# Low parts of the values in the zero columns of their weights, in a cross-attention kernel on one Trainium2 core

## The chip, the cores and the metric

The kernel runs on one core of a Trainium2 chip. The metric is the time on the device in microseconds (us) of one execution; lower is better. The core has TensorE (PE in the rows; PEld is its weight load), VectorE (DVE), ScalarE (ACT), GpSimd (POOL) and the DMA queue of SyncE (SP). Each runs its own list of instructions in order, and semaphores tie the lists together. Before the change the kernel takes 660.38 us, the median of three runs.

## The reference, cut to what matters

The input is 4 batches of 512 tokens of width 1024. A LoRA layer with a router updates them (first phase of the kernel). Then each batch attends to its own 64 vision tokens with 32 heads of width 32, and a layer norm follows:

```python
Q = (hidden_states @ Wq.T + bq).reshape(B, L, NH, HD)
K = (vision_features @ Wk.T + bk).reshape(B, Vn, NH, HD)
Vv = (vision_features @ Wv.T + bv).reshape(B, Vn, NH, HD)
scores = jnp.einsum('blhd,bvhd->bhlv', Q, K) / np.sqrt(HD).astype(np.float32)
scores = jnp.where(mask, scores, -jnp.inf)
attn = jax.nn.softmax(scores, axis=-1)
ctx = jnp.einsum('bhlv,bvhd->blhd', attn, Vv).reshape(B, L, H)
attn_out = ctx @ Wo.T + bo
x = hidden_states + attn_out
# layer norm of x over the 1024 columns, times ln_g plus ln_b
```

All of it is float32. TensorE works here in float32r, which keeps fewer bits, so a product a·b is made of parts: a = a_hi + a_lo, b = b_hi + b_lo, and a_hi·b_hi + a_hi·b_lo + a_lo·b_hi is summed in PSUM: three matmuls for one.

## The kernel before

Two phases are written out as one list of stages that every engine walks (`first_phase`, `second_phase`, `run`). The first phase makes the updated tokens, the queries, the keys and the values, and stores queries, keys, values and output weights, each in high and low parts, in DRAM. The second phase, from about 320 us on, is a software pipeline of 86 steps.

A unit is 256 tokens (8 units), and a chunk is 4 heads (128 columns) of a unit, so a unit has 8 chunks and there are 64 chunks in all. Below, s is the step and c = s mod 8 is its place in a group of eight steps. Chunk n passes these stations:

- scores(n), TensorE, step n+2: queries times the block-diagonal keys, 6 matmuls into one bank (two banks in turn).
- scale_and_min(n), VectorE, step n+2: L921 scales and masks, L926 takes the minima. GpSimd then subtracts (L1220) and ScalarE takes the exponentials (L1138, L1142).
- inverse(n), VectorE, step n+3: sums (L931) and reciprocal (L934). GpSimd multiplies (L1213).
- p_transposed(n), TensorE, step n+5: four transposes (L730). ScalarE makes the high parts p_hi (L1147), VectorE the low parts p_lo (L938).
- context(n), TensorE, step n+6 (L735 to L743): probabilities times values. For each of two pairs g of heads the weights `vbd[:, c, g, :]` are 128 rows (2 heads by 64 vision tokens) by 128 columns. Of these only the 64 columns of the pair's own two heads are filled, 64·g to 64·g+63; the rest stays zero from a memset (L1208). Three matmuls for each g add into the same 256 columns of a bank, so all 128 rows of the result are filled: 6 matmuls.
- ctx_high(n), ScalarE, first in step n+7 (L1156), adds the bias of the values and rounds to cx_hi. ctx_low(n), VectorE (L943), in step n+7 between inverse and p_low, makes cx_lo.

In each step TensorE does scores, p_transposed, half a group of the output projection (12 matmuls of 512 columns, `projection`) and context, in this order. At c = 6 and c = 7 the projection is the first group of the unit whose chunks were last finished. It waits for `clo_done`, the counter of finished cx_lo: at c = 6 for the first four chunks of the unit, at c = 7 for all eight, and the eighth chunk's context was made by TensorE only at c = 5, so its parts are made in step c = 6.

VectorE in each step does L921, L926, L931, L934, L943 and L938. In even steps it adds the output group to the residual (L951, L955); at c = 2 and 6 follow the moments (L959) and at c = 3 and 7 a Newton step in five small instructions (L963 to L977), one of which (L970) multiplies two SBUF tensors. Stages of the layer norm go to ScalarE (L1160, L1163, L1170) and to GpSimd, one in each step (gain L1228, shift L1233), behind its two operations of the softmax. Output groups begin at step 14 and residuals at step 16; chunks end with context(63) in step 69.

Of the kernel before, what the change touches and what calls it, by code (L numbers as in the profile page):

```python
# [5 lines left out]
F32 = mybir.dt.float32  # L6
# [184 lines left out]
def xattn_kernel(nc, xT, ctxT, mask, BT, rW, rb, WqT, WkT, WvT, biases, WoT, ln_g, ln_b, out):  # L191
# [15 lines left out]
    with ExitStack() as ctx:  # L207
# [11 lines left out]
        bias_c = sb("bias_c", [P, 4, KC])  # L219
        bq_c, bk_c, bv_c, bo_c = (bias_c[:, k, :] for k in range(4))  # L220
# [57 lines left out]
        vbd = [at(f"vbd{n}", [P, KC, 2, P], AT_B + 16384 + 8192 * k, F32R) for k, n in enumerate(("_hi", "_lo"))]  # L278
# [24 lines left out]
        ps_v = [ps[:, 0, 0:U], ps[:, 1, 0:U]]  # L303
# [40 lines left out]
        pv_mm, chi_done, clo_done = sem("pv_mm"), sem("chi_done"), sem("clo_done")  # L344
# [21 lines left out]
        def _(sp):  # L366
# [122 lines left out]
            def load_values(b, half):  # L489
                cs = slice(4 * half, 4 * half + 4)  # L490
                for l in range(2):
                    for g in range(2):
                        for s in range(2):
                            sp.dma_start(vbd[l][64 * s:64 * s + 64, cs, g, 64 * g + HD * s:64 * g + HD * s + HD].bitcast(F32),
                                         v_heads[l, b, g, s][:, cs, :]).then_inc(v_in[half], 16)
# [36 lines left out]
            def step(s):  # L532
# [3 lines left out]
                if s in (1, 2):  # L536
                    sp.wait_ge(zeroed, 4)
# [43 lines left out]
        def _(pe):  # L581
# [153 lines left out]
            def context(n):  # L735
# [3 lines left out]
                wait(pe, clo_done, n - 1)  # L739
                if n == 0:  # L740
                    pe.wait_ge(q_copied, ALL - 4)
                three(ps_v[c % 2], [(vbd[0][:, c, g, :], vbd[1][:, c, g, :], p_hi[c % 2][:, g, :], p_lo[c % 2][:, g, :])
                                    for g in range(2)]).then_inc(pv_mm, 1)  # L743
# [33 lines left out]
        def _(dve):  # L777
# [162 lines left out]
            def ctx_low(n):  # L940
                c, u = n % KC, n // KC % 2
                dve.wait_ge(chi_done, n + 1)
                dve.scalar_tensor_tensor(cx_lo[u][:, c, :], ps_v[c % 2], bv_c[:, c:c + 1], cx_hi[u][:, c, :],  # L943
                                         ALU.add, ALU.subtract).then_inc(clo_done, 1)
# [34 lines left out]
            def step(s):  # L979
# [5 lines left out]
                if live(s - 7, CHUNKS):  # L985
                    ctx_low(s - 7)
# [30 lines left out]
        def _(act):  # L1017
# [130 lines left out]

            def ctx_high(n):
                c, u = n % KC, n // KC  # L1150
                act.wait_ge(pv_mm, n + 1)
# [4 lines left out]
                act.activation(cx_hi[u % 2][:, c, :], ps_v[c % 2], ACT.Identity, bias=bv_c[:, c:c + 1]).then_inc(chi_done, 1)  # L1156
# [15 lines left out]
            def step(s):  # L1172
                c = s % KC
                if live(s - 7, CHUNKS):
                    ctx_high(s - 7)
                if live(s - 5, CHUNKS):
                    p_high(s - 5)
                if live(s - 2, CHUNKS):
                    exponential(s - 2)
                for at_c, stage_, n in ((2, inverse_deviation, tile_at(s, 0, 2)), (4, normalise, tile_at(s, 0, 2)),  # L1180
# [10 lines left out]
        def _(pool):  # L1191
# [13 lines left out]
            def zero():  # L1205
                pool.wait_ge(bound_ready, ALL)
                for z in (kbd[0], kbd[1], vbd[0], vbd[1]):
# [77 lines left out]
```

## Time and profile before

| | us |
|---|---|
| median of three runs | 660.38 (660.12 to 660.53) |
| the profiled execution | 661.26 |
| its span, from first to last instruction | 659.5 |
| TensorE busy | 643.9 (98%) |
| VectorE busy | 478.5 (73%) |
| ScalarE busy | 320.4 (49%) |
| GpSimd busy | 204.6 (31%) |

A busy TensorE counts overlapping matmuls as one stretch, so its work is better read from the distance between the starts of its instructions. An instruction's duration is likewise longer than the distance to the next one where the two overlap. A bracket at the end of a row of the timeline is the idle time of the engine before that row and who ended it. The shares over the whole span mix the two phases; those of the second phase are read by windows.

### The profile page before, as it was taken

The page shows a single profiled execution, that of the slowest core. Times are in us where ns is not written, and L with a number is a line of the kernel's source. Part 1 is how long each engine was busy: PE and PEld are TensorE (multiplying, and loading weights), DVE is VectorE, ACT ScalarE, POOL GpSimd, SP SyncE. Part 2 cuts the span into 40 slices and gives each one's busy share as a digit, 9 for nine tenths or more (in the row PEclk, how much of TensorE's full clock was granted, in tenths as well). Part 3 has the DMA queues.
Part 4 walks back from the last instruction along what each step waited for, and adds up shares of the span by engine and source line. Part 5 has one row for each costly group of instructions (what it writes and reads, how often), then busy time and mean ns, then how long its engine had stood idle before and what let it go on. Part 6 is the DMA issues. An engine that isn't in the chain of part 4 may idle for free.

```text
span 659.5 us, 10610 instructions
## 1 busy us (share of the span) xinstructions
PE 643.9 (98%) x3559; PEld 558.7 (85%) x3559; DVE 478.5 (73%) x917; ACT 320.4 (49%) x935; POOL 204.6 (31%) x215
## 2 busy tenths in 40 slices
PE   7999999999999999999999999999999999999995
PEld 6988879888888878888888989898888889888884
DVE  5779985578447773677467777988888888988634
ACT  5453362223242242323267666766676676766411
POOL 0020001100110002000433334666565656656643
PEclk9999999999999999999999999999999999999998
DMA  8936684436883478612866982515444443512311
GB/s 304 378 126 177 178 305 141 176 80 209 244 298 98 109 239 266 261 33 103 227 217 231 413 282 79 172 59 171 113 131 136 132 132 111 176 68 94 129 64 64
DMA packets 103253, 114.12 MB, mean 173 GB/s; under 512 B 56992, under 2 KB 76064, under 8 KB 103200
## 3 DMA queue, kind: packets, MB, share of 16 engines
q1 hardware_dynamic: 103008, 113.20, 52.3%
q8 instruction: 28, 0.46, 0.3%
q10 hardware_dynamic: 192, 0.26, 0.2%
q14 instruction: 25, 0.20, 0.1%
HBM read 67.29 MB, written 46.14 MB: 172 GB/s over the span
## 4 chain that ended last, share of the span: by engine, by line
PE 83%; DVE 11%; DMA 2%; ACT 2%; issue 1%; SPq 1%; DVEq 0%; ACTq 0%
PE ps L585 24%; PE ps L586 24%; PE ps L587 24%; PE ps L647 4%; PE ps L730 4%; DVE w_lo L803 2%; DVE h_t L890 1%; DMA stage<-WkT 1%; DVE x_sb L873 1%; DVE h_t L887 1%; DVE act_lo L858 1%; PE ps L657 1%; DVE q_sb L900 1%; ACT act_hi L1103 1%; DMA x_sb<-xT 1%
## 5 line engine op out<-in xcount | busy, mean ns | idle before, releaser
L585 PE MATMUL ps<-wo_hi,cx_hi 128*128 128x512 f32 x256 | 104.5, 408 | 0.0
L1138 ACT ACTIVATE s_sb<-s_sb,s_min 128x64 f32<-128x64 f32 x256 | 86.1, 337 | 34.2 <-DVE s_min L926 34.2
L585 PE MATMUL ps<-act_hi,w_hi 128*128 128x512 f32 x256 | 100.9, 394 | 1.6 <-DVE kv_sb L813 0.9
L587 PE MATMUL ps<-wo_hi,cx_lo 128*128 128x512 f32 x256 | 100.3, 392 | 0.0
L586 PE MATMUL ps<-wo_lo,cx_hi 128*128 128x512 f32 x256 | 100.2, 391 | 0.0
L586 PE MATMUL ps<-act_lo,w_hi 128*128 128x512 f32 x256 | 99.8, 390 | 0.0
L587 PE MATMUL ps<-act_hi,w_lo 128*128 128x512 f32 x256 | 99.8, 390 | 0.0
L1202 POOL TENSOR_TENSOR u_sb<-a_sb,w_sb 128x512 f32<-128x512 f32 x16 | 18.1, 1153 | 240.7 <-DVE w_sb L847 234.0
L1220 POOL TENSOR_TENSOR s_sb<-s_sb,s_min 128x256 f32<-128x256 f32 x64 | 39.3, 614 | 133.5 <-DVE s_min L926 133.5
L921 DVE SCALAR_TENSOR_TENSOR s_sb<-ps,mask_f 128x512 f32<-128x512 f32 x64 | 44.2, 690 | 46.9 <-PE ps L587 45.4
L1103 ACT ACTIVATE act_hi<-h_t 128x512 fp32r<-128x512 f32 x32 | 20.3, 633 | 114.1 <-DVE h_t L890 114.1
L1213 POOL TENSOR_TENSOR s_sb<-s_sb,s_inv 128x512 f32<-128x512 f32 x64 | 66.9, 1046 | 0.0
L585 PEld LDWEIGHTS ps<-act_hi,w_hi 128*128 128x128 f32 x256 | 48.1, 188 | 12.0 <-issue 1.3
L587 PEld LDWEIGHTS ps<-wo_hi,cx_lo 128*128 128x128 f32 x256 | 48.1, 188 | 10.3
L587 PEld LDWEIGHTS ps<-act_hi,w_lo 128*128 128x128 f32 x256 | 48.1, 188 | 10.2
L586 PEld LDWEIGHTS ps<-act_lo,w_hi 128*128 128x128 f32 x256 | 48.1, 188 | 9.2
L586 PEld LDWEIGHTS ps<-wo_lo,cx_hi 128*128 128x128 f32 x256 | 48.3, 189 | 8.5
L585 PEld LDWEIGHTS ps<-wo_hi,cx_hi 128*128 128x128 f32 x256 | 48.2, 188 | 8.3
L1147 ACT ACTIVATE p_hi<-ps 128x512 fp32r<-128x512 f32 x64 | 38.1, 595 | 29.3 <-PE ps L730 29.1
L585 PE MATMUL ps<-u_hi,b_hi 128*128 128x512 f32 x128 | 49.9, 390 | 0.0
L587 PE MATMUL ps<-u_hi,b_lo 128*128 128x512 f32 x128 | 49.8, 389 | 0.0
L586 PE MATMUL ps<-u_lo,b_hi 128*128 128x512 f32 x128 | 49.8, 389 | 0.0
(117 smaller groups left out, 1514.2 us busy)
## 6 DMA issues: line engine op xcount, KB each, us to landing
q_cols<-q_sb SPq DMA_DIRECT2D x32, 512.0 KB, 3.3
qb<-q_cols SPq DMA_DIRECT2D x64, 256.0 KB, 3.5
x_sb<-xT SPq DMA_DIRECT2D x32, 256.0 KB, 3.3
h_rows<-hn_sb SPq DMA_DIRECT2D x64, 128.0 KB, 3.0
output_weights<-wo_sb SPq DMA_DIRECT2D x32, 256.0 KB, 2.5
z_sb<-h_rows SPq DMA_DIRECT2D x16, 512.0 KB, 4.1
out<-z_sb SPq DMA_DIRECT2D x15, 512.0 KB, 2.8
stage<-WvT SPq DMA_DIRECT2D x8, 512.0 KB, 4.8
```

The lines of the kernel that those rows point to most:

```text
L585: pe.matmul(dst, lh, rh, start=(first and j == 0), stop=False)
L586: pe.matmul(dst, lh, rl, start=False, stop=False)
L587: mm = pe.matmul(dst, ll, rh, start=False, stop=(last and j == n - 1))
L647: mm = pe.matmul(ps_al[:, t, :], x_sb[:, k, t * P:(t + 1) * P], a_rhs[:, k, :], start=(k == 0), stop=(k == KC - 1))
L730: mm = pe.transpose(ps_t[c % 2][:, g, t * P:(t + 1) * P], s_sb[c % 4][:, HPC * t + 2 * g:HPC * t + 2 * g + 2, :].rearrange("p h v -> p (h ...
L921: dve.scalar_tensor_tensor(s_sb[c % 4][:], ps_s[c % 2].rearrange("p (h v) -> p h v", v=V), -SCALE, mask_f[:, n // 16, :].unsqueeze(1).to_b ...
L1103: act.activation(act_hi[:, c, :], h_t[m % 3][:], ACT.Copy).then_inc(hhi_done, 1)
L1138: act.activation(s_sb[c % 4][:, h, :], s_sb[c % 4][:, h, :], ACT.Exp, bias=s_min[c % 2][:, h:h + 1], scale=-1.0, accum_out=s_sum[c % 2][:, ...
L1147: act.activation(p_hi[n % 2][:], ps_t[n % 2], ACT.Copy).then_inc(phi_done, 1)
L1202: pool.tensor_tensor(u_sb[t % 2][:], a_sb[:, t, :].unsqueeze(1).to_broadcast([P, NR, R]), w_sb[:, t, :].unsqueeze(2).to_broadcast([P, NR, ...
L1213: pool.tensor_tensor(s_sb[c % 4][:], s_sb[c % 4][:], s_inv[c % 2][:].unsqueeze(2).to_broadcast([P, TU * HPC, V]), ALU.mult).then_inc(p_rea ...
L1220: pool.tensor_tensor(rest, rest, s_min[c % 2][:, ACT_HEADS:].unsqueeze(2).to_broadcast([P, TU * HPC - ACT_HEADS, V]), ALU.subtract).then_i ...
```

## The change: what it does

The weights of the context hold both parts: for the pair g, the 64 columns that were zero get the low parts of the same values. One pass with p_hi and one with p_lo then give, for each g, the product with the high parts in the 64 rows of that g and the product with the low parts in the other 64 rows. The two pairs no longer add into the same columns but take 256 columns each, so the bank's 512 columns are in use, and 4 matmuls take the place of 6 (the product of both low parts, left out before, is among them).

The two halves have to be added across partitions. In step n+7, ScalarE first copies the whole bank to SBUF (`ctx_copy`, 128x512). VectorE, where ctx_low stood, does `ctx_sum`: two instructions on 64 partitions each. For pair g it reads the high half from PSUM in its own partitions, and the bias and the low half from SBUF in the other 64 partitions, and writes `cx_sum` in its own. ScalarE then rounds `cx_sum` to cx_hi (`ctx_high`, now behind the exponentials of the step), and GpSimd makes cx_lo (`ctx_low`, now last in its step). TensorE's context waits for the sums of chunk n−2 and no longer for its low parts; the projection still waits for `clo_done`. One of four memsets goes, and the DMAs of the values write the same bytes to one tile. On the host the halves of each 128 values of the bias are swapped.

```diff
-        vbd = [at(f"vbd{n}", [P, KC, 2, P], AT_B + 16384 + 8192 * k, F32R) for k, n in enumerate(("_hi", "_lo"))]
+        vbd = at("vbd", [P, KC, 2, P], AT_B + 16384, F32R)
+        cx_raw = [at(f"cx_raw{k}", [P, 2, U], AT_B + 24576 + 2048 * k) for k in range(2)]
+        cx_sum = [at(f"cx_sum{k}", [P, U], AT_B + 28672 + 1024 * k) for k in range(2)]
...
-        ps_v = [ps[:, 0, 0:U], ps[:, 1, 0:U]]
+        ps_v = [ps[:, k, :].rearrange("p (g n) -> p g n", g=2) for k in range(2)]
...
-                            sp.dma_start(vbd[l][64 * s:64 * s + 64, cs, g, 64 * g + HD * s:64 * g + HD * s + HD].bitcast(F32),
+                            col = 64 * (g ^ l) + HD * s
+                            sp.dma_start(vbd[64 * s:64 * s + 64, cs, g, col:col + HD].bitcast(F32),
                                          v_heads[l, b, g, s][:, cs, :]).then_inc(v_in[half], 16)
...
-                wait(pe, clo_done, n - 1)
+                wait(pe, cx_summed, 2 * (n - 1))
...
-                three(ps_v[c % 2], [(vbd[0][:, c, g, :], vbd[1][:, c, g, :], p_hi[c % 2][:, g, :], p_lo[c % 2][:, g, :])
-                                    for g in range(2)]).then_inc(pv_mm, 1)
+                for g in range(2):
+                    pe.matmul(ps_v[c % 2][:, g, :], vbd[:, c, g, :], p_hi[c % 2][:, g, :], start=True, stop=False)
+                    mm = pe.matmul(ps_v[c % 2][:, g, :], vbd[:, c, g, :], p_lo[c % 2][:, g, :], start=False, stop=True)
+                mm.then_inc(pv_mm, 1)
...
-            def ctx_low(n):
-                c, u = n % KC, n // KC % 2
-                dve.wait_ge(chi_done, n + 1)
-                dve.scalar_tensor_tensor(cx_lo[u][:, c, :], ps_v[c % 2], bv_c[:, c:c + 1], cx_hi[u][:, c, :],
-                                         ALU.add, ALU.subtract).then_inc(clo_done, 1)
+            def ctx_sum(n):
+                c = n % KC
+                dve.wait_ge(cx_copied, n + 1)
+                wait(dve, chi_done, n - 1)
+                wait(dve, clo_done, n - 1)
+
+                for g in range(2):
+                    own, other = slice(64 * g, 64 * g + 64), slice(64 - 64 * g, 128 - 64 * g)
+                    dve.scalar_tensor_tensor(cx_sum[n % 2][own, :], ps_v[c % 2][own, g, :], bv_c[other, c:c + 1],
+                                             cx_raw[n % 2][other, g, :], ALU.add, ALU.add).then_inc(cx_summed, 1)
...
+            def ctx_copy(n):
+                act.wait_ge(pv_mm, n + 1)
+                wait(act, cx_summed, 2 * (n - 1))
+                act.activation(cx_raw[n % 2][:], ps_v[n % 2], ACT.Copy).then_inc(cx_copied, 1)
+
             def ctx_high(n):
                 c, u = n % KC, n // KC
-                act.wait_ge(pv_mm, n + 1)
+                act.wait_ge(cx_summed, 2 * n + 2)
...
-                act.activation(cx_hi[u % 2][:, c, :], ps_v[c % 2], ACT.Identity, bias=bv_c[:, c:c + 1]).then_inc(chi_done, 1)
+                act.activation(cx_hi[u % 2][:, c, :], cx_sum[n % 2][:], ACT.Copy).then_inc(chi_done, 1)
...
                 if live(s - 7, CHUNKS):
-                    ctx_high(s - 7)
+                    ctx_copy(s - 7)
                 if live(s - 5, CHUNKS):
                     p_high(s - 5)
                 if live(s - 2, CHUNKS):
                     exponential(s - 2)
+                if live(s - 7, CHUNKS):
+                    ctx_high(s - 7)
...
+            def ctx_low(n):
+                c, u = n % KC, n // KC % 2
+                pool.wait_ge(chi_done, n + 1)
+                pool.tensor_tensor(cx_lo[u][:, c, :], cx_sum[n % 2][:], cx_hi[u][:, c, :], ALU.subtract).then_inc(clo_done, 1)
...
                     if c == at_c and live(n, TILES - 1):
                         stage_(n, half)
+                if live(s - 7, CHUNKS):
+                    ctx_low(s - 7)
```

## Rows read from the trace of the kernel before

**Rows 1.** The page, part 1: busy time, share of the span, instructions.
```profile
PE 643.9 (98%) x3559; PEld 558.7 (85%) x3559; DVE 478.5 (73%) x917; ACT 320.4 (49%) x935; POOL 204.6 (31%) x215
```

**Rows 2.** Windows: length, busy PE, PEld, DVE, ACT, POOL; clock, DMA share, GB/s.
```profile
376.00:380.00 4.00, 4.00 (x27) 3.60 (x27) 3.86 (x8) 3.76 (x18) 2.40 (x3) 1.00 1.02 415
...
460.00:500.00 40.00, 40.00 (x247) 35.81 (x246) 34.16 (x74) 28.02 (x104) 25.52 (x27) 1.00 0.45 130
```

**Rows 3.** Timeline of TensorE, steps c = 2 and 3: start, duration, engine, line.
```profile
485.71 0.60 PE L730 MATMUL ps<-ident,s_sb 128*128 128x128 f32 x4
...
488.90 0.28 PE L585 MATMUL ps<-p_hi,vbd_hi 128*128 128x256 f32 x1
...
489.61 0.28 PE L585 MATMUL ps<-kbd_hi,qb 128*128 128x256 f32 x1
...
490.33 0.60 PE L730 MATMUL ps<-ident,s_sb 128*128 128x128 f32 x4
...
490.69 0.48 PE L585 MATMUL ps<-wo_hi,cx_hi 128*128 128x512 f32 x1
```

**Rows 4.** Timeline of VectorE, steps c = 2 and 3.
```profile
485.91 0.69 DVE L921 SCALAR_TENSOR_TENSOR s_sb<-ps,mask_f 128x512 f32<-128x512 f32 x1 [1.70 <-PE ps L587]
...
487.24 0.41 DVE L931 TENSOR_REDUCE s_sum<-s_sb 128x4 f32<-128x256 f32 x1
487.68 0.20 DVE L934 RECIPROCAL s_inv<-s_sum 128x8 f32<-128x8 f32 x1
487.80 0.43 DVE L943 SCALAR_TENSOR_TENSOR cx_lo<-ps,bias_c,cx_hi 128x256 fp32r<-128x256 f32 x1
488.15 0.68 DVE L938 TENSOR_TENSOR p_lo<-ps,p_hi 128x512 fp32r<-128x512 f32 x1
...
489.47 0.69 DVE L955 BATCH_NORM_STATS2 stats<-z_sb 128x6 f32<-128x512 f32 x1
490.19 0.21 DVE L959 BATCH_NORM_AGGREGATE mv<-stats 128x2 f32<-128x12 f32 x1
490.53 0.69 DVE L921 SCALAR_TENSOR_TENSOR s_sb<-ps,mask_f 128x512 f32<-128x512 f32 x1
...
494.05 0.85 DVE L970 TENSOR_TENSOR rstd<-nudge,guess 128x1 f32<-128x1 f32 x1
494.94 0.21 DVE L977 TENSOR_SCALAR offset<-mv,rstd 128x1 f32<-128x1 f32 x1
```

**Rows 5.** Lines of the source: ns shortest/median/longest, first and last start.
```profile
L943 DVE SCALAR_TENSOR_TENSOR cx_lo<-ps,bias_c,cx_hi x64: 432/433/484, 347.2 to 630.2; 128x256 fp32r<-128x256 f32 x64
...
L970 DVE TENSOR_TENSOR rstd<-nudge,guess x16: 158/856/861, 401.6 to 655.3; 128x1 f32<-128x1 f32 x16
...
L1147 ACT ACTIVATE p_hi<-ps x64: 576/597/602, 337.4 to 622.8; 128x512 fp32r<-128x512 f32 x64
...
L1142 ACT ACTIVATE s_sb<-s_sb x64: 399/403/407, 328.5 to 613.4; 128x256 f32<-128x256 f32 x64
```

**Rows 6.** Timeline of GpSimd, steps c = 2 and 3.
```profile
487.40 0.61 POOL L1220 TENSOR_TENSOR s_sb<-s_sb,s_min 128x256 f32<-128x256 f32 x1 [1.75 <-DVE s_min L926]
487.97 1.05 POOL L1213 TENSOR_TENSOR s_sb<-s_sb,s_inv 128x512 f32<-128x512 f32 x1
488.98 1.29 POOL L1228 TENSOR_TENSOR z_sb<-z_sb,g_b 128x512 f32<-128x512 f32 x1
...
493.59 1.29 POOL L1233 TENSOR_TENSOR z_sb<-z_sb,lb_b 128x512 f32<-128x512 f32 x1
```

**Rows 7.** Timeline of the first phase: GpSimd, then VectorE, in the same stretch.
```profile
31.74 3.03 POOL L1202 TENSOR_TENSOR u_sb<-a_sb,w_sb 128x512 f32<-128x512 f32 x2 [30.24 <-DVE w_sb L847]
...
31.98 3.87 DVE L803 TENSOR_TENSOR b_lo<-stage,b_hi 128x1024 fp32r<-128x1024 f32 x2 [0.33 <-ACT b_hi L1050]
```

**Rows 8.** Timeline of TensorE at the scores of step 16.
```profile
383.08 0.28 PE L587 MATMUL ps<-p_hi,vbd_lo 128*128 128x256 f32 x1
383.25 0.39 PE L585 MATMUL ps<-kbd_hi,qb 128*128 128x256 f32 x1
```

More of the change, by code:

```diff
@@ L343, in xattn_kernel @@
         pt_mm, phi_done, plo_done = sem("pt_mm"), sem("phi_done"), sem("plo_done")
-        pv_mm, chi_done, clo_done = sem("pv_mm"), sem("chi_done"), sem("clo_done")
+        pv_mm, cx_copied, cx_summed = sem("pv_mm"), sem("cx_copied"), sem("cx_summed")
+        chi_done, clo_done = sem("chi_done"), sem("clo_done")
         o_mm, z_ready, bn_done, ag_done = sem("o_mm"), sem("z_ready"), sem("bn_done"), sem("ag_done")
@@ L536, in step @@
                 if s in (1, 2):
-                    sp.wait_ge(zeroed, 4)
+                    sp.wait_ge(zeroed, 3)
                     load_values(0, s - 1)
@@ L985, in step @@
                 if live(s - 7, CHUNKS):
-                    ctx_low(s - 7)
+                    ctx_sum(s - 7)
                 if live(s - 5, CHUNKS):
@@ L1206, in zero @@
                 pool.wait_ge(bound_ready, ALL)
-                for z in (kbd[0], kbd[1], vbd[0], vbd[1]):
+                for z in (kbd[0], kbd[1], vbd):
                     pool.memset(z[:].bitcast(F32), 0.0).then_inc(zeroed, 1)
@@ L1265, in by_blocks, with by_halves @@
         return a.reshape(*a.shape[:-1], P // B, KC, B).swapaxes(-3, -2).reshape(a.shape)
+    def by_halves(a):
+        return np.asarray(a).reshape(KC, 2, P // 2)[:, ::-1].reshape(H)
     arrays = {
@@ L1274 @@
         "biases": lay(np.stack([np.asarray(b).reshape(KC, P) for b in
-                                (L1_xattn_bq, L1_xattn_bk, L1_xattn_bv, by_blocks(L1_xattn_bo))]), 2, 0, 1),
+                                (L1_xattn_bq, L1_xattn_bk, by_halves(L1_xattn_bv), by_blocks(L1_xattn_bo))]), 2, 0, 1),
         "WoT": lay(L1_xattn_Wo, 1, 0),
```

## The prediction

> **What bounds the kernel now.** I read the page's busy shares first, then the second phase by windows, then one stretch of two steps on each engine's timeline. TensorE is busy for 98% of the span [rows 1] and for 40.00 of 40.00 us in the middle of the second phase, where VectorE has 34.16 and GpSimd and ScalarE about two thirds [rows 2]. The reader should see two things there. TensorE has no idle time at all, so each matmul that goes is time that can come out. And VectorE, at 85% of the same window, is next: TensorE may get faster by about a seventh at most before VectorE is the bound, and this change loads VectorE.
>
> One step of TensorE is 4.62 us, transposes to transposes (485.71 to 490.33), of which the six context matmuls take 488.90 to 489.61: 0.71, or 0.118 each [rows 3]. Eight steps (a unit) take 36.96.
>
> VectorE's part of a step: 2.24 from its first instruction to p_low, which lasts 0.68; residual steps go on to the end of L955 at 4.25; at c = 2 and 6 the moments end at 4.49; at c = 3 and 7 the Newton step ends at 4.62 [rows 4]. Measured to the next possible start, each is about 0.08 shorter, since an instruction that depends on nothing may start 0.08 before the one ahead ends (reciprocal 487.68 + 0.20, next start 487.80). Four steps: 4.17 + 2.84 + 4.41 + 4.54 = 15.96; a unit: 31.9 of 36.96. The idle 1.70 ahead of 485.91 is that slack [rows 4].
>
> **What the change removes.** Two of six context matmuls in each of 64 steps: 2 x 0.118 = 0.237, so a step of TensorE is 4.38, a unit 35.06, and all 64 are worth 15.2 us if nothing else ends last. The copies, the rounding and GpSimd's part have room as work. ScalarE is busy 28.02 of 40 [rows 2], 3.24 a step; it gains a copy of 128x512 from PSUM, priced like L1147 (0.60), and the rounding now reads SBUF (like L1142, 0.40) instead of 0.46 from PSUM [rows 5]: 3.8 of 4.4. GpSimd has 25.52 of 40, 2.95 a step, and gains a subtraction of 128x256 that no row shows in this form: at least 0.61 (L1220, same size with a broadcast) and at most 1.29 (L1228, twice the size) [rows 6]. I take 1.29 x 0.61 / 1.05 = 0.75, the size scaled as L1220 to L1213. That makes 3.7. The new waits between them: VectorE's sums wait for the copy, with p_low and the residual queued behind; copy and L1147 are 1.2 us of work at the head of ScalarE's step, and the sums come at 2.0. ScalarE's rounding waits for the sums, with the layer norm and the next copy behind; the sums are done at 3.0, before the exponentials are.
>
> **What it costs VectorE.** One instruction of 256 columns becomes two, also of 256 columns; half the partitions should save nothing. No row shows an instruction that starts on other partitions than its neighbours, so the price is bounded. If the two overlap as L943 does now, the second adds its distance, 488.15 − 487.80 = 0.35 [rows 4]. If none of the three changes of partitions (reciprocal to first sum, first to second, second to p_low) lets the next start before the last has ended, then each start waits for the end plus about 0.035 (L931 at 487.24, 0.41 long, to its dependent at 487.68) [rows 4]. From the reciprocal's start to p_low it is 0.47 now. It becomes 0.24 + 0.47 + 0.47 = 1.18 with a sum of 0.43, or 1.28 with 0.48, the longest L943, which started behind idle time [rows 5]. The extra is 0.71 to 0.82. I take 0.76: the pairs that overlap in the rows all start on partition 0, so they say least about these three, and a gain below nothing is excluded, since an instruction is added.
>
> The Trainium skill, "VectorE: DVE Perf Modes", section "Two Vector instructions with no wait between them", has a rule here. An instruction is held until all earlier ones have finished when its operand or output starts in another group of 32 partitions than the last one used in that memory. By it the three holds are certain and the sum is the one with 0.76; without it the sum would be the first rival's. No row of before can show it.
>
> The extra counts in full at c = 0, 1, 2, 4, 5, 6. At c = 3 and 7 it is mostly absorbed: L970, which lasts 0.158 alone, now takes 0.856 [rows 5], and at c = 3 it ends at 494.90, when GpSimd's shift ends (493.59 + 1.29) [rows 4, 6]. It waits for that operation. Coming 0.76 later, at 4.28 into its step, it would end at 4.44 instead of 4.37: +0.07. VectorE's unit is then 31.9 + 6 x 0.76 + 2 x 0.07 = 36.6. That is more than TensorE's 35.06: VectorE becomes the bound, and a unit gains 0.36 us, not 1.9.
>
> **Where TensorE waits.** At c = 7 the projection needs the low parts made in step c = 6, and the chain there is longer: copy, sums, rounding behind the exponentials, then GpSimd last in its step. From VectorE's start of the step GpSimd ends its gain at 490.27 − 485.91 = 4.36 [rows 4, 6]. Its subtraction starts 0.04 before that, as its operations now follow each other, and ends at 5.07; the rounding is done well before, at about 3.6. TensorE wants it one step plus 0.16 after that start (490.69 against 490.53) [rows 3, 4]: 4.38 + 0.13 = 4.51, with 0.06 for the signal. So there is a stall of 0.62 plus whatever VectorE lags behind. Queued behind that wait on TensorE are the rest of the projection, the context and the next scores. In the first unit with residuals (steps 16 to 23) the lag grows by 0.55 at c = 0 (4.17 + 0.76 − 4.38), falls by 0.78 at c = 1 and so to nothing, grows by 0.79 and 0.23 at c = 2 and 3, and after c = 4 and 5 is 0.79 at c = 6: a stall of 1.4 and a unit of 36.47. After that VectorE never idles and a unit is 36.6, of which 1.54 is this stall.
>
> **The sum**, against the profiled execution of 661.26 us:
> - Steps 6 to 15, no residuals: VectorE has room (2.92 + 0.76 against 4.38), so 10 x 0.237 = 2.4 comes out. Against it, the scores of step 16 start 0.17 after the matmul before them instead of 0.12, and take 0.39 instead of 0.28 [rows 8], with the DMA engines full (1.02) just before [rows 2]: I read that as the queries' load only just landing. TensorE would come 2.4 earlier; the load follows only in part. Between 0 and 2.4 is lost; I take 1.0, nearer to nothing because the weights' loads ahead of it are released by TensorE's progress. Net 1.4.
> - Steps 16 to 63: 0.49 + 5 x 0.36 = 2.3.
> - Steps 64 to 69: 6 x 0.237 = 1.4; VectorE is light again. At step 71 the last chunk's chain (0.60, 0.48, 0.48, 0.40, 0.75 and five signals of about 0.05: 2.95) meets a half group of about 2.8 less the overlap of the last matmul: 0.4 lost. Net 1.0.
> - The memset that goes and the regrouped DMAs cost or bring nothing: TensorE works through that stretch on queries.
>
> Together 4.7: 656.6 for the profiled execution. That one stood 0.9 above the median of its runs, so the median goes to 655.7.
>
> **Rivals.**
> First, the sums overlap like the rest. Then VectorE's unit is about 31.9 + 6 x 0.35 = 34.0 and it has slack; TensorE's is 35.06 plus the bare stall of 0.62, 35.7. For it: every independent pair in the rows overlaps. Against it: none of those pairs changes partitions. Saved: 1.4 + 6 x 1.26 + 1.0 = 10.0, so 650.4.
>
> Second, and slower: the arbitration at L970. In the changed kernel GpSimd has its new subtraction queued directly behind the shift at c = 3 and 7. If GpSimd keeps its turn, L970 waits for both and ends at 5.07 instead of 4.44: +0.63 twice a unit, 1.26, and over six units 7.5, which gives 663.2. It decides from 0.8 us a unit on. Against it stands one place in the first phase. Two GpSimd operations of about 1.04 each were queued together from 31.74 and took 3.03 in all, with VectorE's two-input L803 starting at 31.98 [rows 7]: VectorE got in between the two.
>
> Third, four matmuls take as long as six, because something other than their count sets the pace. Then TensorE keeps 36.96 and gains a stall of about 0.3 a unit: 662. The distances are so even at 0.118 that I give it little.
>
> **How the numbers follow.** Forecast 0.60, first rival 0.20, second 0.12, third 0.03, and 0.05 for an extra on VectorE above 0.85, where the unit passes 36.96 by more than the other steps bring. Within the forecast, an extra of 0.71 gives a unit of 36.2 and 653.4, one of 0.82 gives 37.1 and 658.5, and the load of the queries moves it by 1 more: 652.4 to 659.5. The range reaches down to the first rival and a little above the forecast's own: 649.8 to 661.0. A measurement of this kernel can tell about 0.2% (1.3 us) from no change. Faster by more than that (below 659.1): 0.57 of the forecast and 0.20 less a little, so 0.73. Within: 0.12. Slower: 0.12 and 0.03 from the second and third rivals and the tail, 0.15.
>
> **What would show it.** In the changed kernel's profile: context matmuls still 0.12 apart, four in a step; on VectorE the reciprocal's start to p_low's at 1.2 to 1.3 us (0.8 would be the first rival), and no idle time ahead of L921 in the units with residuals; one wait of TensorE a unit at c = 7, of 1.3 to 1.7 us, for GpSimd's low part (0.6 under the first rival); L970 ending within 0.1 of the shift's end (0.7 later under the second); and 36.6 us from unit to unit. The prediction is wrong above all if the three changes of partitions cost other than 0.71 to 0.82 together: each 0.1 there moves the time by about 4.

## The result, and the profile after

The changed kernel takes 668.82 us (median of 4 runs, 668.29 to 669.21), the kernel before 660.25 (4 runs, 659.72 to 660.53): a ratio of 1.013, 95% interval 1.012 to 1.015. It is slower, where 655.7 was forecast. The profiled execution took 668.49 us, its span is 666.7 us against 659.5.

The page of the changed kernel, parts 1 and 5, answers to [rows 1]:

```profile
PE 636.1 (95%) x3431; PEld 546.6 (82%) x3431; DVE 519.1 (78%) x981; ACT 339.9 (51%) x999; POOL 248.5 (37%) x278
...
L592 PE MATMUL ps<-wo_hi,cx_hi 128*128 128x512 f32 x256 | 106.8, 417 | 16.2 <-POOL cx_lo L1247 16.2
```

TensorE is busy 7.8 us less, for 128 matmuls fewer, and stands idle for 16.2 us ahead of the output projection, waiting for GpSimd's low parts. That is half of the 15.1 that 128 x 0.118 make. Part of the rest went back in at a lower clock, as the windows show (columns as in [rows 2]):

```profile
380.00:382.00 2.00, 2.00 (x7) 1.52 (x7) 1.89 (x5) 1.57 (x9) 1.52 (x2) 0.59 1.07 327
382.00:384.00 2.00, 2.00 (x7) 1.57 (x6) 0.69 (x1) 0.48 (x2) 0.82 (x2) 0.55 1.07 347
456.00:458.00 2.00, 2.00 (x5) 1.62 (x6) 1.90 (x6) 1.91 (x7) 0.60 (x2) 0.50 0.94 317
458.00:460.00 2.00, 2.00 (x8) 1.57 (x8) 1.90 (x5) 1.50 (x8) 2.00 (x3) 0.78 0.10 39
...
460.00:500.00 40.00, 38.24 (x230) 33.73 (x229) 37.75 (x81) 28.66 (x104) 29.44 (x34) 1.00 0.44 126
```

In the window of 40 us VectorE went from 34.16 [rows 2] to 37.75 and TensorE from 40.00 to 38.24. VectorE has no idle time there to speak of (of the 2.25 us, 0.26 stand at 461.48, right behind a stretch at the lower clock, and the rest are gaps of about 0.04 between its instructions), so it is the bound. The first four windows have a granted clock of 0.50 to 0.78: in each of them it stood for a part or all of the time at 0.5, which is the 1.2 GHz level.

TensorE's timeline at c = 6 and 7, which answers to [rows 3]:

```profile
490.75 0.28 PE L750 MATMUL ps<-p_hi,vbd 128*128 128x256 f32 x1
490.87 0.28 PE L751 MATMUL ps<-p_lo,vbd 128*128 128x256 f32 x1
490.99 0.28 PE L750 MATMUL ps<-p_hi,vbd 128*128 128x256 f32 x1
491.11 0.28 PE L751 MATMUL ps<-p_lo,vbd 128*128 128x256 f32 x1
491.23 0.28 PE L592 MATMUL ps<-kbd_hi,qb 128*128 128x256 f32 x1
...
491.95 0.60 PE L737 MATMUL ps<-ident,s_sb 128*128 128x128 f32 x4
494.31 0.51 PE L592 MATMUL ps<-wo_hi,cx_hi 128*128 128x512 f32 x1 [1.76 <-POOL cx_lo L1247]
```

Four context matmuls 0.12 apart, and one wait at c = 7. VectorE's timeline at c = 7, and GpSimd's beside it, answer to [rows 4] and [rows 6]:

```profile
494.45 0.65 DVE L930 SCALAR_TENSOR_TENSOR s_sb<-ps,mask_f 128x512 f32<-128x512 f32 x1
...
496.19 0.20 DVE L943 RECIPROCAL s_inv<-s_sum 128x8 f32<-128x8 f32 x1
496.42 1.00 DVE L957 SCALAR_TENSOR_TENSOR cx_sum<-ps,bias_c,cx_raw 64x256 f32<-64x256 f32 x2
497.45 0.69 DVE L947 TENSOR_TENSOR p_lo<-ps,p_hi 128x512 fp32r<-128x512 f32 x1
...
498.74 0.74 DVE L984 TENSOR_TENSOR rstd<-nudge,guess 128x1 f32<-128x1 f32 x1
...
499.65 0.68 DVE L930 SCALAR_TENSOR_TENSOR s_sb<-ps,mask_f 128x512 f32<-128x512 f32 x1
...
497.48 1.29 POOL L1259 TENSOR_TENSOR z_sb<-z_sb,lb_b 128x512 f32<-128x512 f32 x1
498.73 0.73 POOL L1247 TENSOR_TENSOR cx_lo<-cx_sum,cx_hi 128x256 fp32r<-128x256 f32 x1
```

From the reciprocal to p_low it is 1.26 us. L984, the product that was L970, starts 4.29 us into the step, within 0.01 us of GpSimd's subtraction, and ends with it: 0.74 us for an operation of one element per row. So it is in 11 of its 16 places. The lines of the source answer to [rows 5]:

```profile
L957 DVE SCALAR_TENSOR_TENSOR cx_sum<-ps,bias_c,cx_raw x128: 477/483/490, 346.1 to 637.5; 64x256 f32<-64x256 f32 x128
...
L984 DVE TENSOR_TENSOR rstd<-nudge,guess x16: 158/747/1217, 403.8 to 662.5; 128x1 f32<-128x1 f32 x16
...
L1247 POOL TENSOR_TENSOR cx_lo<-cx_sum,cx_hi x64: 719/737/748, 347.7 to 638.5; 128x256 fp32r<-128x256 f32 x64
```

Last, TensorE's timeline at two places behind such a wait, with the transposes that open a step:

```profile
376.79 0.60 PE L737 MATMUL ps<-ident,s_sb 128*128 128x128 f32 x4
379.71 0.51 PE L592 MATMUL ps<-wo_hi,cx_hi 128*128 128x512 f32 x1 [2.31 <-POOL cx_lo L1247]
...
380.64 0.63 PE L592 MATMUL ps<-wo_hi,cx_hi 128*128 128x512 f32 x1
381.06 0.63 PE L593 MATMUL ps<-wo_lo,cx_hi 128*128 128x512 f32 x1
...
455.80 0.80 PE L592 MATMUL ps<-wo_hi,cx_hi 128*128 128x512 f32 x1 [2.66 <-POOL cx_lo L1247]
...
457.25 0.63 PE L592 MATMUL ps<-wo_hi,cx_hi 128*128 128x512 f32 x1
457.68 0.63 PE L593 MATMUL ps<-wo_lo,cx_hi 128*128 128x512 f32 x1
...
461.28 0.60 PE L737 MATMUL ps<-ident,s_sb 128*128 128x128 f32 x4
```

Behind the waits of 2.31 and 2.66 us the matmuls stand 0.42 and 0.43 apart and last 0.63, where at the upper level they stand 0.23 apart and last 0.39.

By the transposes that open each step, the span divides so (us; a gain is positive):

| stretch | before | after | measured | forecast |
|---|---|---|---|---|
| up to step 5 (code that doesn't differ) | 335.89 | 334.93 | +0.96 | 0 |
| steps 5 to 14 | 43.41 | 41.86 | +1.55 | +1.4, with step 15 |
| step 15 | 4.77 | 8.57 | −3.80 | |
| steps 16 to 63 | 221.76 | 227.63 | −5.87 | +2.3 |
| from step 64 to the end | 53.67 | 53.71 | −0.04 | +1.0 |

The six units from step 16 on took 36.52, 39.40, 37.11, 37.94, 39.57 and 37.09 us, before always 36.96.

In some executions of any of these kernels the granted clock also falls in the first phase, in code that the experiments leave alone (an example stands with e5); the ratios leave out executions more than 1.5% above the fastest of the same kernel, and where times scatter I compare the loop, from the first transposes to the last.

### The profile page after: what moved, and what is told of

Same layout as the page of the kernel before. It is cut to its first block, busy times and chain, and to the rows that moved or that the text cites. A ratio compares the mean times of both kernels' runs of the same rounds, so it can differ in the third digit from the quotient of the medians.

```text
span 666.7 us, 10669 instructions
## 1 busy us (share of the span) xinstructions
PE 636.1 (95%) x3431; PEld 546.6 (82%) x3431; DVE 519.1 (78%) x981; ACT 339.9 (51%) x999; POOL 248.5 (37%) x278
## 4 chain that ended last, share of the span: by engine, by line
PE 49%; DVE 34%; issue 9%; ACT 2%; POOL 2%; DMA 2%; SPq 1%; DVEq 0%; ACTq 0%
PE ps L592 13%; PE ps L594 13%; PE ps L593 13%; DVE cx_sum L957 5%; DVE s_sb L930 5%; DVE p_lo L947 4%; PE ps L654 4%; DVE s_sum L940 3%; DVE z_sb L965 2%; DVE w_lo L812 2%; DVE h_t L899 1%; DVE stats L969 1%; DVE rstd L984 1%; DVE x_sb L882 1%; DVE h_t L896 1%
## 5 line engine op out<-in xcount | busy, mean ns | idle before, releaser
L592 PE MATMUL ps<-wo_hi,cx_hi 128*128 128x512 f32 x256 | 106.8, 417 | 16.2 <-POOL cx_lo L1247 16.2
L594 PE MATMUL ps<-wo_hi,cx_lo 128*128 128x512 f32 x256 | 102.1, 399 | 0.0
L593 PE MATMUL ps<-wo_lo,cx_hi 128*128 128x512 f32 x256 | 101.8, 397 | 0.0
L957 DVE SCALAR_TENSOR_TENSOR cx_sum<-ps,bias_c,cx_raw 64x256 f32<-64x256 f32 x128 | 61.8, 483 | 6.4 <-ACT cx_raw L1166 2.1
L930 DVE SCALAR_TENSOR_TENSOR s_sb<-ps,mask_f 128x512 f32<-128x512 f32 x64 | 43.3, 676 | 17.1 <-PE ps L594 16.9
L1247 POOL TENSOR_TENSOR cx_lo<-cx_sum,cx_hi 128x256 fp32r<-128x256 f32 x64 | 47.2, 737 | 10.3 <-ACT cx_hi L1175 10.3
```

What stands on the lines that cost most here:

```text
L592: pe.matmul(dst, lh, rh, start=(first and j == 0), stop=False)
L593: pe.matmul(dst, lh, rl, start=False, stop=False)
L594: mm = pe.matmul(dst, ll, rh, start=False, stop=(last and j == n - 1))
L930: dve.scalar_tensor_tensor(s_sb[c % 4][:], ps_s[c % 2].rearrange("p (h v) -> p h v", v=V), -SCALE, mask_f[:, n // 16, :].unsqueeze(1).to_b ...
L957: dve.scalar_tensor_tensor(cx_sum[n % 2][own, :], ps_v[c % 2][own, g, :], bv_c[other, c:c + 1], cx_raw[n % 2][other, g, :], ALU.add, ALU.a ...
L1247: pool.tensor_tensor(cx_lo[u][:, c, :], cx_sum[n % 2][:], cx_hi[u][:, c, :], ALU.subtract).then_inc(clo_done, 1)
```

## The experiments

| kernel | time, us (lowest to highest) | loop, us | usual unit | waits for GpSimd's low parts |
|---|---|---|---|---|
| before | 660.25 (659.72 to 660.53) | 286.6 | 36.96 | none |
| after | 668.82 (668.29 to 669.21) | 293.7 | 37.1 to 39.6 | 16.2 |
| e1_four_alone | 646.29 (646.05 to 647.27) | 273.2 | 35.04 | none |
| e2_same_partitions | 652.57 (650.95 to 665.80) | 279.3 | 35.63 | 4.2 |
| e3_rstd_scalar | 660.88 (659.48 to 665.98) | 287.3 | 36.92 | 11.8 |
| e4_six_matmuls | 668.82 (668.08 to 669.61) | 294.1 | 38.0 | 5.9 |
| e5_filled_wait | 669.16 (665.13 to 678.05) | 290.9 | 38.0 | 8.4 |
| e6_low_first | 670.93 (666.84 to 674.80) | 293.2 | 38.0 | 14.7 |
| e7_newton_gpsimd | 653.04 (651.55 to 654.43) | 278.3 | 35.63 | 4.5 |
| e8_both | 649.74 (648.10 to 654.83) | 276.3 | 35.04 | 2.6 |
| e9_both_filled | 648.33 (647.83 to 661.13) | 274.8 | 35.04 | 1.2 |
| b1_before_newton | 660.71 (659.71 to 673.15) | 286.4 | 36.96 | none |

The loop, the units and the waits (us of idle time) are those of the profiled execution. The times are medians of 4 to 12 executions.

**e1, TensorE's part alone.** The four matmuls stay; VectorE makes the low parts in one instruction as before, and nothing is copied or summed, so the low halves are missing from the result.

```
-    dve.scalar_tensor_tensor(cx_sum[...][own, :], ps_v[...][own, g, :], ..., cx_raw[...][other, g, :], ...)   (twice)
+    dve.scalar_tensor_tensor(cx_lo[u][:, c, :], ps_v[c % 2][:, 0, :], bv_c[:, c:c + 1], cx_hi[u][:, c, :], ...)
```

> TensorE's part alone: four context matmuls in place of six, while ScalarE rounds and VectorE subtracts one half of the bank straight from PSUM as in the kernel before; the low halves are never added, so that part of the computation is left out. Theory (VectorE's list became the bound, the matmuls did go): TensorE's step is 4.38 us throughout, the full 15.2 us come out less about 1 for the queries' load, 645 to 647 us. Rival (the two matmuls are not worth 0.237 a step, or the loads eat them): above 650.

Measured: 646.29 us, ratio 0.979 (0.978 to 0.981). Every unit takes 35.04, eight steps of 4.38. All of TensorE's waits in the loop:

```profile
PE ps L592 <- DMA qb<-q_cols: 1.4, 1, 1.4
PE ps L750 <- DVE p_lo L947: 0.4, 1, 0.4
```

So two matmuls fewer in each step are worth 13.4 us of the loop, against 15.2 by their count; the load below takes most of the rest. What the change loses, it loses in the work that it gives the other engines. The one wait that is new is the queries' load, ahead of the scores of step 16.

**e2, the sums without a change of partitions.** Both sums run over 128 partitions from partition 0, each in its own output; the halves are not added.

```
-    scalar_tensor_tensor(cx_sum[own, :], ps_v[own, g, :], bv_c[other], cx_raw[other, g, :], ...)
+    scalar_tensor_tensor(cx_sum[:, g, :], ps_v[:, g, :], bv_c, cx_raw[:, g, :], ...)
```

> The whole new chain, but both sums of VectorE start on partition 0 with all their operands and outputs (128 partitions each), so the halves are not added to each other and this part of the result is left out. Theory (the change of partitions keeps the sums from overlapping their neighbours): from the reciprocal's start to p_low's 0.82 us in place of 1.27, VectorE's unit about 34 us, TensorE's 35.1 plus one wait of 0.5 to 0.8: 649 to 652 us. The product of two SBUF tensors in the Newton step then comes about 0.4 us before GpSimd's shift ends: if a waiting VectorE goes between two GpSimd operations it lasts about 0.5 us, if GpSimd keeps its turn about 1.2. Rival (the second instruction costs 0.5 wherever it starts): 1.27 stays and the time is that of the changed kernel, 668.

Measured: 652.57 us, ratio 0.990 (0.987 to 0.993), 0.6 over the range of the theory. VectorE, then GpSimd, at c = 3 or 7 of this kernel:

```profile
488.70 0.20 DVE L943 RECIPROCAL s_inv<-s_sum 128x8 f32<-128x8 f32 x1
488.82 0.87 DVE L956 SCALAR_TENSOR_TENSOR cx_sum<-ps,bias_c,cx_raw 128x256 f32<-128x256 f32 x2
489.60 0.68 DVE L947 TENSOR_TENSOR p_lo<-ps,p_hi 128x512 fp32r<-128x512 f32 x1
...
490.88 0.43 DVE L983 TENSOR_TENSOR rstd<-nudge,guess 128x1 f32<-128x1 f32 x1
...
490.00 1.30 POOL L1258 TENSOR_TENSOR z_sb<-z_sb,lb_b 128x512 f32<-128x512 f32 x1
491.25 0.73 POOL L1246 TENSOR_TENSOR cx_lo<-cx_sum,cx_hi 128x256 fp32r<-128x256 f32 x1
```

With twice the partitions the two sums cost less: 0.90 from the reciprocal to p_low (0.82 was expected) instead of 1.27. The difference of 0.37 in each of eight steps is the price of the changes of partitions. It does not touch the wait at step 15: that is still 2.26 us. And here the product comes 0.37 sooner, finds GpSimd in the middle of the shift, and ends at 491.31, when the shift ends, although the subtraction is queued directly behind it. VectorE gets in between two GpSimd operations if it is already waiting.

**e3, the product with a scalar operand.** Same result: the second tensor of one element per row becomes a per-partition scalar.

```
-    dve.tensor_tensor(rstd[:], nudge[:], guess[:], ALU.mult)
+    dve.tensor_scalar(rstd[:], nudge[:], guess[:, 0:1], 1.0, ALU.mult, ALU.mult)
```

> The changed kernel with one edit: the last product of the Newton step takes its second factor as a scalar per partition, not as a second SBUF tensor. Theory (VectorE's list is the bound and twice a unit it waits there for GpSimd): that instruction falls from 0.74 to about 0.2 us, a unit of eight steps from 38.0 to 36.9, and with shorter waits TensorE's clock falls less often: 658 to 663 us. Rival (TensorE's wait for the low parts is a matter of GpSimd's chain, not of VectorE's list): 667 to 669.

```profile
L984 DVE TENSOR_SCALAR rstd<-nudge,guess x16: 212/214/215, 403.5 to 654.8; 128x1 f32<-128x1 f32 x16
```

Measured: 660.88 us, ratio 1.002 (1.000 to 1.004). No product waits any more, VectorE's unit is 36.92 instead of 38.0, and 8 us come back. So one wait of 0.53 us, twice in a unit, cost with what follows from it about as much as the change lost: of the 6.4 us that the loop is shorter, some 5 are the shorter units, and 1.2 are clock falls in the units, of which this execution has none. That is no gain over the kernel before yet: its unit is 36.96. The Trainium skill, "SBUF — State Buffer", section "Who interferes with whom", says that a VectorE instruction with two SBUF inputs contends with a GpSimd instruction that reads SBUF. The traces agree: with GpSimd's subtraction starting at the same moment, the product takes 0.74 us with two tensors and 0.21 with one.

**e4, six matmuls again, with the same result.** The pass with p_hi is made twice.

```
+    pe.matmul(ps_v[c % 2][:, g, :], vbd[:, c, g, :], p_hi[c % 2][:, g, :], start=True, stop=True)
     pe.matmul(ps_v[c % 2][:, g, :], vbd[:, c, g, :], p_hi[c % 2][:, g, :], start=True, stop=False)
```

> The changed kernel with TensorE's saving given back: the pass with the high probabilities is made twice for each pair, the second time over the first, so six matmuls and the same result. Theory (VectorE's list is the bound in steps 16 to 63): only the steps without residuals pay, 16 x 0.237 = 3.8 us, and TensorE's waits shrink by 1.9 a unit, so that the clock falls less: 667 to 672 us. Rival (TensorE's work still counts in full): 15.2 more, 684.

Measured: 668.82 us, ratio 1.013 (1.012 to 1.015), the same as the changed kernel to 0.1 us. TensorE has its 15 us of work again, the time is in the range of the theory, its waits shrink by 10.3, and the clock falls are gone:

```profile
PE ps L592 <- POOL cx_lo L1248: 5.9, 7, 1.9
```

So the changed kernel as it stands gets nothing for TensorE's saving: units stay at 38.0, VectorE's pace, from the second on. No wait is over 1.9 us. But the saving is not worth nothing by itself. Against e5, which keeps it and has no clock falls either, e4's loop is 3.2 us longer (294.1 against 290.9), near the 3.8 that the theory gave the steps without residuals; in the changed kernel the clock falls eat 2.8 of it.

**e5, the waits filled with matmuls.** Six matmuls whose result is thrown away stand ahead of the wait at c = 7.

```
+    if o % 4 == 0 and part == 1 and o < 28:     (in every unit but the last)
+        ... (a wait for VectorE, so that the bank is free)
+        for _ in range(6):
+            pe.matmul(ps_s[(s - 3) % 2], wo_hi[0][:, 0:P], wo_hi[0][:, 0:HALF], start=True, stop=True)
     pe.wait_ge(clo_done, KC * (o // 4) + 4 * part + 4)
```

> The changed kernel, with six more matmuls of 512 columns on TensorE just ahead of its wait for GpSimd's low parts at c=7 in every unit but the last (their result is thrown away; they lie in the time in which TensorE waited: six of 0.23 are 1.4 us, the waits there were 1.2 to 2.7). The question is what the clock falls cost. After the waits of 2.31, 2.66 and 2.68 us the granted clock was about 0.5 for some 3 us, and the units with a fall took 39.40 and 39.57 us where the others took 36.5 to 37.9. Theory, the falls cost what the units show: with the wait filled the clock stays at its upper level, all units from step 24 on take about 38.0 (the pace of VectorE), the step behind s=15 takes 4.4 and some tenths more, and the time is 663 to 665.5. Rival, VectorE sets the pace anyway and a slow TensorE behind the wait costs nothing: 668 to 669.5. Second rival, the fillers are in the way because they hold TensorE when the low parts arrive: up to 8 times some tenths above the rest, over 669.5.

Measured: 669.16 us over four scattered runs (665.13, 665.60, 672.72, 678.05), so one in the range of the theory, one 0.1 over it and two far above; ratio 1.012 (1.006 to 1.017). TensorE's timeline at a wait, and windows of the first phase and of the loop:

```profile
463.68 1.64 PE L760 MATMUL ps<-wo_hi 128*128 128x512 f32 x6
466.56 0.50 PE L592 MATMUL ps<-wo_hi,cx_hi 128*128 128x512 f32 x1 [1.24 <-POOL cx_lo L1252]
...
160.00:180.00 20.00, 19.16 (x97) 17.52 (x97) 9.10 (x16) 4.38 (x7) 0.00 (x0) 0.76 0.77 237
...
390.00:400.00 10.00, 9.07 (x49) 7.49 (x49) 8.35 (x18) 7.48 (x31) 5.60 (x8) 1.00 1.05 374
```

The profiled execution lost its time before the loop, at a clock of 0.76 around 170 us, in code that is the same in this kernel and the changed one. From the medians nothing can be concluded. The loop can be compared, since the clock stayed at its upper level in it: 290.9 us against 293.7. No fall is left in it, step 15 takes 7.00 instead of 8.57, and the units from the second on 37.94 to 38.01. The falls cost 2.8 us, of which 1.57 at step 15 and 1.2 over the six units. That is less than the 3.3 to 5.8 that the theory put down: behind a fall TensorE's next unit is short (37.11, 37.09), because VectorE, which sets the pace, was held up much less. From its own L930 to L930 the two units from each fall on took 38.33 and 38.17, and 38.47 and 38.17, where e5 has 37.97 to 37.99: 0.5 and 0.7 us lost.

**e6, the low parts ahead of the gain.** GpSimd's order at c = 2 and 6 is turned round.

```
+    if live(s - 7, CHUNKS) and c in (2, 6):
+        ctx_low(s - 7)
     for at_c, stage_, n, half in (... gain ..., shift ...):
```

> The changed kernel with GpSimd's order turned round at c=2 and c=6: the low parts of the context, for which TensorE waits at the step after, stand ahead of the multiplication by the gain (1.3 us) instead of behind it. High parts are there 1.9 us into VectorE's step at c=6, the low parts start 2.7 us into it, so they can be ready 0.8 us sooner. Theory, VectorE has no idle time and its unit of 37.99 us is what is repeated: the sooner low parts give TensorE 0.8 us once and it waits the same sum elsewhere, 667 to 668.6 if the clock falls stay, and 662.5 to 665 if shorter waits (1.5 to 1.9 us in place of 2.3 to 2.7) keep the clock up. Rival, the wait for the low parts is what sets the unit: 8 times 0.8 us less, 662 or, with the falls gone too, 657 to 659.

Measured: 670.93 us (four scattered runs, 666.84 the lowest), ratio 1.016 (1.010 to 1.022); the loop is 293.2, 0.5 under the changed kernel. By the time that is outside both ranges of the theory and above the rival's, by the loop it is the theory with the falls left. The first unit is 0.74 shorter (35.78), after that units are 38.0 again, the last 39.56 with a clock fall. The waits did not shrink to the expected 1.5 to 1.9 either: in a usual unit TensorE still waits 2.31 us for the low parts, and loses another 0.35 in the step before. What TensorE waits for by name isn't what limits it: make that sooner, and VectorE's pace makes it wait as long.

**e7, the small operations on GpSimd.** The three operations on nudge, the product and the offset move from VectorE to the start of GpSimd's steps c = 3 and 7.

```
-    (3, newton, tile_at(s, 0, 2)) ... (7, newton, tile_at(s, 1, 2))     on VectorE
+    pool.tensor_scalar(nudge, ...) x3; pool.tensor_tensor(rstd, ...); pool.tensor_scalar(offset, ...)
```

> The changed kernel with the five operations of one element per row behind the statistics (three on nudge, the product rstd, the offset) on GpSimd, at the start of its steps c=3 and c=7, in place of VectorE. On VectorE they took 1.59 us from the end of the low parts of p to the next scaling, twice in a unit (of it 0.53 for the product that starts with GpSimd's cx_lo). Theory, VectorE's load is the cause of all that was lost: its unit goes from 37.99 to about 34.8, under TensorE's 35.04 (8 steps of 4.38), which becomes the bound again; no clock falls from step 24 on, what is left over e1 (646.3) is the queue at c=7 with GpSimd's low parts behind: 647 to 652. Rival, what is added to GpSimd takes the place: five small operations with a wait between each, if they take over 0.3 us each, put its subtraction of the minimum at c=3 and c=7 late and with it the exponentials: 655 to 662. Second rival, contention of GpSimd and VectorE stretches other operations of VectorE by as much: over 664.

Measured: 653.04 us, ratio 0.990 (0.987 to 0.992): 15.8 under the changed kernel, 1 over the range of the theory. GpSimd's timeline:

```profile
469.58 0.26 POOL L1243 TENSOR_SCALAR nudge<-mv,guess 128x1 f32<-128x1 f32 x1 [0.92 <-ACT guess L1174]
469.95 0.27 POOL L1245 TENSOR_SCALAR nudge<-nudge,guess 128x1 f32<-128x1 f32 x1
...
470.88 0.26 POOL L1252 TENSOR_SCALAR offset<-mv,rstd 128x1 f32<-128x1 f32 x1
471.10 0.61 POOL L1233 TENSOR_TENSOR s_sb<-s_sb,s_min 128x256 f32<-128x256 f32 x1
```

The five take 1.56 us on GpSimd, in a place where it had been idle for 1.6. VectorE isn't the bound any more. The unit is 35.63 and not 35.04, since TensorE still waits once in each for the low parts. That wait shows as 0.33 us of idle time, but by the starts of its instructions the step c = 7 takes 4.98 instead of 4.38: idle time is counted only from the end of the matmul before, which overlaps with the next where nothing waits.

**e8, both.**

> Both of the last two together: the small operations on GpSimd and the context's low parts ahead of the gain at c=2 and c=6. With VectorE at 34.8 us in a unit and TensorE at 35.04 neither has to wait for the other on average, and what is left is the phase between them. Theory, the wait of TensorE for the low parts at c=7 is then a real one, repeated in each unit, and sooner low parts shorten it: 0.5 to 3 us under the kernel with the small operations alone, 646.5 to 650. Rival, it is a wait that happens once at the start of the loop and then no more: within 0.5 us of the kernel with the small operations alone.

Measured: 649.74 us, ratio 0.985 (0.981 to 0.990). That is in the range of the theory by its time, and 3.3 under e7 where at most 3 was expected. Windows of it:

```profile
380.00:384.00 4.00, 4.00 (x13) 3.15 (x13) 2.27 (x6) 2.05 (x10) 2.35 (x3) 0.61 1.07 344
...
460.00:500.00 40.00, 40.00 (x238) 35.46 (x237) 38.21 (x76) 31.77 (x117) 35.10 (x48) 1.00 0.49 145
```

TensorE is busy for 40.00 of 40.00 again and a unit is 35.04. The edit that brought 0.5 us to the loop when VectorE was the bound brings 6 x 0.59 = 3.5 in the units now; of the loops' difference 2.0 is left, because this execution has a clock fall at step 15 (8.53 against 6.96) and e7's had none behind the same wait of 2.31.

**e9, the one wait that is left filled.** Six matmuls as in e5, at step 15 alone.

> The kernel with the small operations on GpSimd and the low parts ahead of the gain (e8), with six more matmuls of 512 columns on TensorE (result thrown away) ahead of the one wait that was left, at step 15. There TensorE stood for 2.31 us and the granted clock fell behind it; from the transposes of step 15 to those of step 16 it took 8.53 us, and 7.00 in the kernel in which six such matmuls lay in that wait. Theory, the clock follows TensorE's own idle time: no fall, the step takes 7.0, and the time is about 1.5 us under 649.7: 647.5 to 649. Rival, the fall only hides behind VectorE, which is late at this place: 649.3 to 650.2.

Measured: 648.33 us, ratio 0.984 (0.981 to 0.988). Step 15 takes 6.96 instead of 8.53 us and the loop 274.8 instead of 276.3, as the theory has it. The medians differ by 1.4, but the runs of the two overlap, so the loop carries this verdict. It is the fastest version that computes the whole output, 1.6% under the kernel before.

**b1, the kernel before with the small operations on GpSimd.** As e7, on the kernel before.

> The kernel before (six matmuls for the context, VectorE making the low parts), with nothing changed but the five small operations behind the statistics, which GpSimd does instead of VectorE, as in e7. It tells whether the gain of e8 over the kernel before is that of the small operations alone. Theory, TensorE bounds the kernel before (8 steps of 4.62 us are its unit of 36.96), so relieving VectorE brings nothing but the short lag at the start of the loop: 658.5 to 660.5, and the gain of e8 needs both, fewer matmuls and a relieved VectorE. Rival, VectorE already sets the pace of the kernel before somewhere: 2 us less or more, under 658.

Measured: 660.71 us, ratio 1.002 (1.000 to 1.004), units of 36.96. That is 0.2 over the range of the theory and rules out the rival: relieving VectorE brings nothing there. The gain of e8 is that of the fewer matmuls, and it appears when VectorE has room for their price.

## Why the prediction was wrong

**What bounds, and TensorE's side: right.** Four matmuls 0.12 apart, a step of 4.38, units of 35.04 wherever nothing else is late (e1, e8). The bare stall at c = 7 was right too: 0.62 forecast, 0.6 by the starts in e2 and e7, where VectorE has slack. The third rival, matmuls that take as long as six, is out.

**The price on VectorE: right.** 1.18 to 1.28 was forecast from the reciprocal to p_low, 1.26 to 1.27 was measured, each sum 0.48 long and 0.04 to the next start. The extra was 0.80, in the range of 0.71 to 0.82, near its upper end. e2 shows that the changes of partitions are the cause: 0.37 us a step. Eight steps at 0.04 over the value taken are 0.3 us of unit. The Trainium skill, "VectorE: DVE Perf Modes", section "Two Vector instructions with no wait between them", has the rule on held instructions that the prediction weighed; the traces agree with it, 1.26 us with the three changes and 0.90 without.

**L970 at c = 3 and 7: the step that failed.** The prediction let it wait for the shift, +0.07. It reckoned its arrival right, 4.28 into the step. For c = 6 it put the start of GpSimd's new subtraction 0.04 before the end of the gain, 4.32 into the step, and the shift of c = 3 and 7 ends at about the same place; but it never laid the one beside the other: L984 arrives just as the subtraction starts and waits for the whole of it, 0.74. The second rival named the place, the price (1.26 a unit; e3 gives 1.08) and the direction (its total of 663.2 is still 5.6 under what was measured), but argued it as GpSimd keeping its turn, and so ruled it down to 0.12 by [rows 7]. Those rows were read rightly: e2 shows VectorE getting in between. It was a question of who comes first: with its arrival 0.37 us ahead of the subtraction the product got in, with a tie it did not. How close it may come is not shown, for no run lies between the two. Both terms together make VectorE's unit: 36.6 + 0.3 + 1.1 = 38.0, as measured in e4 and e5 (without the second it is 36.9, as measured in e3). Those 38.0 are over the 36.96 of the kernel before, which is the sign of the result: 5 x 1.04 lost behind a first unit of 36.5 that gained 0.44, so 4.8 lost (4.6 in e5) where 2.3 gained was forecast.

**Step 15: a lag that was left out.** The prediction gave VectorE room in all steps 6 to 15, from their mean. But TensorE's step 13, with neither queries nor projection, lasts only 1.63 us (transposes at 370.47 and 372.10), and VectorE needs 3.64, with the last two tiles of the queries (L909) still ahead of it:

```profile
370.40 1.41 DVE L909 SCALAR_TENSOR_TENSOR q_sb<-ps,bias_c,q_sb 128x512 fp32r<-128x512 f32 x2 [0.37 <-ACT q_sb L1123]
371.72 0.68 DVE L930 SCALAR_TENSOR_TENSOR s_sb<-ps,mask_f 128x512 f32<-128x512 f32 x1
...
375.36 0.68 DVE L930 SCALAR_TENSOR_TENSOR s_sb<-ps,mask_f 128x512 f32<-128x512 f32 x1
...
378.92 0.73 POOL L1247 TENSOR_TENSOR cx_lo<-cx_sum,cx_hi 128x256 fp32r<-128x256 f32 x1 [0.47 <-ACT cx_hi L1175]
```

So VectorE began its step 14 at 375.36, 3.26 behind TensorE's transposes: 1.25 from the tiles and 2.01 from the short step. The low parts were ready 4.29 later, and the wait of 2.31 that ends at 379.71 is the consequence. It takes the lag and the longer chain together: e1 lags by 2.2 at this place (373.88 against 371.71), but has neither sums nor GpSimd's part, and no such wait. The pieces by runs: step 15 would take 4.38; with the queries' load alone 6.04 (e1, in which the wait of 1.4 for qb shows it; 1.0 was taken, of at most 2.4); with VectorE's lag, which covers the load, 7.00 (e5); with the clock fall 8.57. Before it took 4.77.

**The clock: not in the sum at all.** [rows 1] to [rows 3] show a TensorE without idle time, and a wait of up to 1.7 was forecast. Nothing was charged for what comes behind a wait. By e5 it cost 2.8 us in the profiled execution.

**Small terms.** The first unit came out at 36.52 (forecast 36.47), with a wait of 1.20 at its end, 1.48 by the starts (1.4). In the sum for that wait the prediction put 0.13 where its rows give 0.16 (490.69 − 490.53); that is 0.03. At step 71 the wait was 1.18 instead of the 0.4 lost; that and 0.2 that I didn't trace make the last stretch come out even instead of 1.0 better. The start of the loop came 0.96 sooner. After 20 us TensorE was already 1.3 ahead, where it had waited less for the parts of the first weights. That has nothing to do with the change: in b1, whose first phase is that of the kernel before, the loop starts as early (334.87).

Put together against the forecast of 4.7 gained: steps 16 to 63 came out 8.2 worse (6.9 by VectorE's unit, 1.2 by the clock), steps 6 to 15 3.7 worse, the end 1.0 worse, the start 1.0 better. That is 11.9, and 4.7 − 11.9 = −7.2, the difference of the spans.

## What to carry over

When a change moves a bound from one engine to the next, cost the next one to the hundredth at each place where it meets a third. Lay the arrival of every VectorE instruction with two SBUF tensors beside the start of each GpSimd operation: here a tie cost the whole operation, and the instruction with one tensor input didn't pay it. Ask of each idle engine what small work it can take before giving up such a change: here 1.6 us of idle GpSimd, twice a unit, turned 1.3% slower into 1.0% faster (e7), and 1.5% with the low parts ahead of the gain (e8). And where a loop has steps of unlike length, reckon the lag step by step, not by the mean.

## What the runs showed of the hardware

- The granted clock fell to its lower level behind TensorE's waits of 2.31, 2.66 and 2.68 us, for some 3 us, and did not behind those of 1.20, 1.76 and, once, 2.64. In e2, e3, e6 and e8 it fell behind the wait of 2.3 at step 15, in e7 not. In e6 five units have the same wait of 2.31, and only the last of them brought a fall. Filling the wait with matmuls kept the clock up in all of e5's units and in e9's loop. The fall began between 0.3 us before the end of the wait and 1.5 us behind it. So the length of a wait alone doesn't decide it; what does isn't settled here.
- The sums of VectorE that start on other partitions than the instruction before do not overlap with it: 64x256 sums that change take 0.48 + 0.04 us each, 128x256 sums that don't change 0.39 (0.78 from the first to p_low, for two). Half the partitions saved nothing, and the change cost.
- VectorE's instruction of one element per row with two tensors took 0.16 us alone, 0.43 when it came 0.43 before the end of GpSimd's shift, 0.74 when it came with the start of GpSimd's subtraction, and 1.22, once, when it came just behind the start of a shift; the one with one tensor 0.21 in all 16 places.
- The small operations last 0.19 to 0.27 us on GpSimd and start 0.29 to 0.36 apart, against 0.15 to 0.21 on VectorE, 0.19 to 0.25 apart.
